# Two attention layers and two Fourier layers on one core: contraction over 192 channels as 128 + 64 rows

## The chip, the cores and the metric

The kernel runs on one core of a Trainium2 chip, in one launch. The metric is the device time of an execution in microseconds (us); of several executions the median is given. A profile is one further execution, taken by the hardware profiler. Engines: PE (TensorE, matmuls; PEld is its weight load), DVE (VectorE), ACT (ScalarE), POOL (GpSimd), SP (SyncE, here only the issuer of copies).

## The reference

An image x of shape (8, 16, 16, 192) goes through four layers. Two attention layers (in the style of a windowed vision transformer), then two layers that mix channels in the Fourier domain. The change touches the attention layers only, one of which is, shortened:

```python
h = layernorm(x) * n1_w + n1_b
win = window_partition(pad(h), 14)                  # 16x16 padded to 28x28: 4 windows of 14x14 = 196 tokens
q, k, v = split(win @ qkv_w + qkv_b)                # 12 heads of 16 channels
attn = (q * 0.25) @ k.T + rel_h[..., None] + rel_w  # relative positions: q @ rel_pos_h, q @ rel_pos_w
out = softmax(attn) @ v
x = x + unpartition(out @ proj_w + proj_b)[:, :16, :16]
mlp = gelu((layernorm(x) * n2_w + n2_b) @ lin1_w + lin1_b) @ lin2_w + lin2_b    # 192 -> 768 -> 192
return x + mlp
```

Padded positions have q, k and v equal to the bias, and as keys they count in the softmax.

## The kernel before, in words

**Jobs and steps.** The eight images are four pairs of 512 tokens. A job is one pair in one attention layer, so there are 8 jobs (layer 0 for jobs 0 to 3, layer 1 for 4 to 7). Within a job the attention runs in 36 steps: 9 units (3 groups of four heads x 3 windows: the two full windows of 196 tokens, and the 120 tokens of the cut windows) of four heads each. The tokens are put in the order of the windows when they are written to SBUF (`pieces`, L135). A step makes scores for one head on PE (`scores`, L911, 8 steps ahead), takes the row maximum on DVE (`row_max`, L516), makes the transposed scores on PE (`scores_T`, L944), exponentials on ACT (`exps`, L707, into PT), and once per unit the values product (`values`, L958), in which four heads use four groups of 32 columns of the array. The maxima of a unit are transposed on PE into bank 5 (`transpose_max`, L934), copied on DVE (`copy_max`, L529) and sent by ACT as one or two small copies into a row of `q_aug` (`send_max`, L744).

**The rest of a job is laid between the steps by hand.** Job m's steps carry the preparation of job m+1 (normalise, transpose, q/k/v projections, relative-position terms) and the end of job m-1 (output projection, second norm, MLP). The step numbers stand in L46 to L57; `build`'s four engine programs (DVE from L590, ACT from L779, PE from L1055, POOL from L421) walk the same step list. All engines are in order, so an instruction that waits holds back everything behind it on its engine. Work between the steps uses two PSUM banks in turn (`free_bank`, L131; `front_free`, L835, waits until a bank's former use is read). Banks 0 and 1 hold scores, 2 and 3 transposed scores, 4 the values product, 5 the transposed maxima and the transposed output.

**Contraction over 192 channels.** Every product over the 192 channels is two matmuls of 96 rows, one of them of 97 where a row of ones adds the bias: `project` (L865; q and k as two tiles of 96 columns each, and in the first job of a layer also the padding keys, `pads_in`, L1038), `values_in` (L900, seven token tiles, the last two or three with padding), `project_out` (L990) and `up` (L1013, six tiles of 128 hidden units). All matmuls with fp32 operands are issued as two instructions, so 8 `project` matmuls stand in the trace as 16 instructions; scores and transposed scores are fp32r and one instruction each.

**Evacuations.** q and k are split into a high and a low part: ACT writes the high part (`q_high`, `k_high`, L656, L664), DVE the difference (`q_low`, `k_low`). POOL adds both again for the relative-position product (`sum_q`, L393; `bias`, L877, 16 matmuls of 32 output rows per axis and group of six heads; `transpose_bias`, L891; `r_high`, `r_low`). ACT writes v (`copy_v`, L698). For the MLP ACT loads the Gelu table, makes two Gelus and loads the Exp table again, three times per job (L796).

**Copies.** SP copies the parts of q, k and of the relative-position terms from their tiles into `q_aug` and `k_aug`, where a head's terms lie on separate partitions, per pair of heads: 4 copies of q, 4 of k, 4 of bias per pair (`send`, L326), 72 per job, and 4 per pair for the padding keys in the first job of a layer. SP first waits until the steps of the former job are done with those heads. The weights for the end of a job are held once for both layers; `load_back(1)` (L274) loads layer 1's after all copies for job 5 and after job 3's last matmuls, and one semaphore counts all seven loads.

**Start and end.** Before job 0's steps the loads, the first norm, the projections and the copies for job 0 run one after another (L342 to L356 on SP); after job 7's steps its own end runs with nothing beside it (L1099). Then the Fourier part (`fourier`, L1116) runs, about 99.5 us; the change doesn't touch it.

Of the kernel before, what the change touches and what calls it, by code (L numbers as in the profile page):

```python
# [6 lines left out]
ALU = mybir.AluOpType  # L7
# [16 lines left out]
G = 2  # L24
HG = NH // G
TILES = TOK // 128
RT = 2 * WS - 1
RK = WS * HG
SUB = HG // 2
# [16 lines left out]
V_AT = (35, 0, 1, 2)  # L46
X_AT = 3
Q_AT, K_AT = (5, 15), (7, 16)
B_AT = ((9, 13), (18, 22))
BT_AT = ((10, 14), (21, 25))  # L50
P_AT = (29, 30)
O_AT = 8
PROJ_AT = (11, 12)
Y_AT = 17
UP_AT = (19, 20, 23, 24, 27, 28)
DOWN_AT = (31, 32, 33, 34)
STATS_AT = (19, 23, 27)  # L57
BIAS_ORDER = ("h a w", "w h a")
V_TILES = [(0, 1), (2, 3), (4, 5), (6,)]
# [17 lines left out]

def first_of_layer(n):
    return n % PAIRS == 0


def free_bank_uses():

    uses = []

    def front(n, wanted):
        uses.extend((n, use) for use in wanted.split())

    pads = lambda n, use: use if first_of_layer(n) else ""
    front(0, "x0 x1 q0 k0 p0 h0 H0 w0 W0 q1 k1 p1 h1 H1 w1 W1 v0")  # L90
    for m in range(JOBS + 1):
        now, more, past = m < JOBS, m + 1 < JOBS, m >= 1
        if now:
            front(m, "v1 v2 v3")
        if more:
            front(m + 1, "x0 x1 q0 k0")
        if past:
            front(m - 1, "t0 t1")
        if more:
            front(m + 1, "h0 H0")  # L100
        if past:
            front(m - 1, "o0 o1")
        if more:
            front(m + 1, "w0 W0 q1 k1")
        if past:
            front(m - 1, "y0 y1")
        if more:
            front(m + 1, "h1")
        if past:
            front(m - 1, "u0 u1")  # L110
        if more:
            front(m + 1, "H1 w1")
        if past:
            front(m - 1, "u2 u3")
        if more:
            front(m + 1, "W1")
        if past:
            front(m - 1, "u4 u5")
        if more:
            front(m + 1, pads(m + 1, "p0 p1"))  # L120
        if past:
            front(m - 1, "d0 d1 d2 d3")
        if more:
            front(m + 1, "v0")
    return uses
# [5 lines left out]
def free_bank(n, use):  # L131
    return 6 + FREE.index((n, use)) % 2
# [34 lines left out]
def attention(nc, d, x_all, bank, consts):  # L167
    with ExitStack() as ctx:
# [3 lines left out]
        def sem(name):  # L172
# [4 lines left out]
        w_qkv = [sb(f"w_qkv{l}", [97, G, 3 * C]) for l in range(2)]  # L177
        w_rel = [sb(f"w_rel{l}", [96, 2 * RT * HG]) for l in range(2)]
        w_proj = sb("w_proj", [97, G, C])
        w_up = sb("w_up", [96, G, MLP])  # L180
# [3 lines left out]
        affine = [sb(f"affine{l}", [96, 4, G]) for l in range(2)]  # L184
# [18 lines left out]
        negT = sb("negT", [8, 4, CUT], F32R)  # L203
# [3 lines left out]
        yT = sb("yT", [97, G, TOK])  # L207
# [6 lines left out]
        names = ("stats1 stats2 aggr1 aggr2 veps1 veps2 rstd1 rstd2 xn1 xn2 xT_mm xT_dve xT_act q_mm q_hi q_lo q_nat "  # L214
                 "k_mm k_hi k_lo p_mm p_hi p_lo r_tok rt_copy r_mm r_hi r_lo v_mm v_copy s_mm max nt_mm negT st_mm exp pv "
                 "o_copy ot_mm inv_sum o_tok oT_mm oT_dve oT_act proj x1 x1b x2_mm x2_dve x2_act up gelu down out").split()
        S = {k: sem(k) for k in names}
        PER = dict(stats1=2, stats2=2, aggr1=1, aggr2=1, veps1=1, veps2=1, rstd1=1, rstd2=1, xn1=1, xn2=1, xT_mm=2,
                   xT_dve=1, xT_act=1, q_mm=2, q_hi=2, q_lo=2, q_nat=2, k_mm=2, k_hi=2, k_lo=2, r_tok=4, rt_copy=4, r_mm=4, r_hi=4, r_lo=4,
                   v_mm=4, v_copy=4, s_mm=STEPS, max=STEPS, nt_mm=UNITS, negT=UNITS, st_mm=STEPS, exp=STEPS,  # L220
                   pv=UNITS, o_copy=UNITS, ot_mm=3, inv_sum=3, o_tok=3, oT_mm=2, oT_dve=1, oT_act=1, proj=2, x1=2, x1b=1,
                   x2_mm=2, x2_dve=1, x2_act=1, up=MC, gelu=MC, down=4, out=4)
        ld_x = [sem(f"ld_x{p}") for p in range(PAIRS)]
        ld_front = [sem(f"ld_front{l}") for l in range(2)]
        ld_static = sem("ld_static")
        ld_back = [sem(f"ld_back{l}") for l in range(2)]
# [4 lines left out]
        q_in = [sem(f"q_in{j}") for j in range(NH // 2)]  # L231
        k_in = [sem(f"k_in{j}") for j in range(NH // 2)]
        r_in = [sem(f"r_in{j}") for j in range(NH // 2)]
        p_in = [sem(f"p_in{j}") for j in range(NH // 2)]
# [3 lines left out]
        PRESETS = 7  # L238
        SENT = 16 * 4
        LD_FRONT, LD_BACK, LD_STATIC = 16 * 4, 16 * 7, 16 * 3  # L240
# [9 lines left out]
        def neg_count(U):  # L250
            return 16 * sum(1 if window(k) == 2 else 2 for k in range(U % 4, U + 1, 4))
# [8 lines left out]
        def _(sp):  # L260
# [6 lines left out]

            def load_front(l):
# [5 lines left out]
            def load_back(l):  # L274
                if l:
                    need(sp, "proj", PAIRS - 1, 2)
# [14 lines left out]
            def rows_of(j, size):  # L291
                return size * (j % SUB), size * (j % SUB) + size
# [1110 lines left out]
```

## Time and profile before

| what | value |
|---|---|
| median of 3 runs | 760.63 us (760.5 to 761.8) |
| the profiled execution's own time | 765.32 us |
| its span, first to last instruction | 763.4 us |
| mean granted TensorE clock | 0.939 of 2.4 GHz |
| PE busy | 650.4 us (85%) |
| DVE, ACT, POOL busy | 351.1, 369.8, 114.9 us |
| bytes moved by copies | 47.4 MB, mean 62 GB/s |

In the profile a row of the timeline gives the start in us from the span's start, the time from the group's first start to its last end, the engine, the line, the operation, the tiles (out<-in), the shape and the count, and in brackets how long the engine had been idle and what released it. PE's matmuls are pipelined: a matmul's own duration is longer than the distance to the next one, so the cost of a stream is read from the length of a group. SPq and ACTq are the issuing of copies by SP and ACT. A row of a stretch gives its window, its length in us, the busy us of each engine (with the instructions it completed where they are given), the granted clock and what the copies moved. The stretches run from the first exponential of one job to that of the next (56.05, 127.77, ..., 412.14, 495.35, 565.60); the last exponential of job 7 ends near 624.

### The profile page before, as it was taken

How to read it: one execution, taken by the hardware profiler on the slowest of the kernel's cores; microseconds unless marked ns; L12 is line 12 of the kernel's file. 1: busy time of each engine (PE TensorE's matmuls, PEld its weight loads, DVE VectorE, ACT ScalarE, POOL GpSimd, SP SyncE). 2: the span in 40 equal slices, each digit the busy share in tenths (PEclk: the TensorE clock that was granted, in tenths of full speed). 3: DMA queues.
4: the chain of work that ended last, by engine and by line, in shares of the span. 5: the costliest groups of instructions: out<-in, count | busy, mean ns of one | idle time of the engine just before them, and what ended most of it. 6: DMA issues, size and time to landing. Idle time of an engine off the chain costs nothing. (4 is left out here: it accounts for less than half of the span.)

```text
span 763.4 us, 15089 instructions
## 1 busy us (share of the span) xinstructions
PE 650.4 (85%) x5592; PEld 486.9 (64%) x5592; DVE 351.1 (46%) x961; ACT 369.8 (48%) x869; POOL 114.9 (15%) x161
## 2 busy tenths in 40 slices
PE   2754598998999999899989598999898877799996
PEld 1333467756875777597659375876597464577774
DVE  3242354654473457335644363356337212156664
ACT  3312254567446555745573336455834741145452
POOL 3120002112020202020220020202001001132231
PEclk9977699999999999999999889999999996989998
DMA  8323233433232135323332522133321000000000
GB/s 207 78 59 91 61 78 81 112 81 70 64 76 66 39 78 133 81 48 76 78 84 48 140 55 60 31 76 79 74 48 40 2 1 0 0 1 22 22 21 21
DMA packets 39342, 47.37 MB, mean 62 GB/s; under 512 B 11852, under 2 KB 20366, under 8 KB 39270
## 3 DMA queue, kind: packets, MB, share of 16 engines
q1 hardware_dynamic: 38310, 46.21, 25.2%
q8 instruction: 46, 0.75, 0.4%
q10 hardware_dynamic: 960, 0.20, 0.1%
q14 instruction: 26, 0.21, 0.1%
HBM read 7.05 MB, written 1.57 MB: 11 GB/s over the span
## 5 line engine op out<-in xcount | busy, mean ns | idle before, releaser
L713 ACT ACTIVATE PT<-bank 98x392 f32<-98x392 f32 (+1 forms) x288 | 136.9, 482 | 179.3 <-PE bank L954 177.8
L525 DVE TENSOR_REDUCE neg_max<-bank 98x2 f32<-98x392 f32 x192 | 105.7, 559 | 70.5 <-PE bank L930 70.0
L954 PE MATMUL bank<-q_aug,k_aug 127*98 127x196 f32 (+1 forms) x672 | 115.2, 265 | 17.9 <-ACT PT L713 16.8
L930 PE MATMUL bank<-k_aug,q_aug 126*98 126x196 f32 x384 | 99.2, 342 | 25.4 <-DMA q_aug<-st_r 15.6
L954 PEld LDWEIGHTS bank<-q_aug,k_aug 127*98 127x98 f32 (+1 forms) x672 | 90.3, 173 | 26.2 <-ACT PT L713 19.7
L1019 PE MATMUL bank<-yT,w_up 96*128 96x512 f32 x192 | 99.7, 649 | 6.6 <-DVE st_r L513 5.6
L930 PEld LDWEIGHTS bank<-k_aug,q_aug 126*98 126x98 f32 x384 | 57.3, 172 | 62.3 <-issue 56.1
L523 DVE TENSOR_REDUCE neg_max<-bank 120x1 f32<-120x318 f32 x96 | 45.7, 484 | 67.1 <-PE bank L926 66.8
L873 PE MATMUL bank<-xT,w_qkv 96*96 96x512 f32 (+3 forms) x144 | 69.5, 611 | 1.9 <-ACT xT L653 1.4
L1028 PE MATMUL bank<-w_down,hidden 128*128 128x192 f32 x384 | 68.9, 331 | 1.0 <-ACT hidden L741 0.9
L391 POOL TENSOR_TENSOR rstd<-veps,half_pow 128x4 f32<-128x4 f32 x16 | 16.4, 1024 | 321.1 <-DVE veps L448 321.1
L1028 PEld LDWEIGHTS bank<-w_down,hidden 128*128 128x128 f32 x384 | 61.7, 190 | 4.2 <-issue 2.2
L968 PE MATMUL bank<-PT,v_aug 98*32 98x196 f32 (+1 forms) x1344 | 63.0, 312 | 0.6 <-ACT PT L713 0.6
L1019 PEld LDWEIGHTS bank<-yT,w_up 96*128 96x128 f32 x192 | 35.7, 204 | 36.3 <-issue 28.5
L513 DVE TENSOR_TENSOR st_r<-bank,st_r 84x392 fp32r<-84x392 f32 (+2 forms) x96 | 26.1, 325 | 67.7 <-ACT st_r L695 67.7
L398 POOL TENSOR_TENSOR q_nat<-st_q 96x392 f32<-96x392 f32 (+2 forms) x48 | 24.9, 545 | 207.5 <-DVE st_q L493 207.5
L759 ACT ACT_TABLE_LOAD x43 | 55.2, 1283 | 0.8
L568 DVE TENSOR_TENSOR x_all<-bank,x_all 128x192 f32<-128x192 f32 x32 | 11.4, 358 | 77.6 <-PE bank L1028 77.6
L926 PE MATMUL bank<-k_aug,q_aug 126*120 126x318 f32 x96 | 46.6, 485 | 0.6 <-DVE neg_max L525 0.4
L907 PE MATMUL bank<-w_qkv,xT 97*98 97x192 f32 (+1 forms) x224 | 44.2, 338 | 0.0
L968 PEld LDWEIGHTS bank<-PT,v_aug 98*32 98x32 f32 (+1 forms) x1344 | 34.3, 110 | 11.2 <-ACT PT L713 1.0
L873 PEld LDWEIGHTS bank<-xT,w_qkv 97*96 97x96 f32 (+1 forms) x144 | 22.8, 176 | 27.7 <-issue 25.5
(87 smaller groups left out, 904.3 us busy)
## 6 DMA issues: line engine op xcount, KB each, us to landing
q_aug<-st_q SPq DMA_DIRECT2D x192, 64.0 KB, 2.0
k_aug<-st_k SPq DMA_DIRECT2D x192, 64.0 KB, 2.0
q_aug<-st_r SPq DMA_DIRECT2D x192, 56.0 KB
x_all<-in_x SPq DMA_DIRECT2D x4, 384.0 KB, 7.2
q_aug<-negT ACTq DMA_DIRECT2D x96, 1.5 KB
out<-y_out SPq DMA_DIRECT2D x4, 384.0 KB, 2.6
k_aug<-st_p SPq DMA_DIRECT2D x48, 24.8 KB, 1.9
w_up<-in_up_w SPq DMA_DIRECT2D x2, 576.0 KB
```

Source lines behind the costliest of these rows:

```text
L523: ins = v.tensor_reduce(neg_max[0:CUT, U % 4, e:e + 1], b[0:CUT, 0:CUT + PADS], AX.X, ALU.max, negate=True)
L525: ins = v.tensor_reduce(neg_max[0:HALF, U % 4, e:e + 5:4], b[0:HALF, 0:2 * WIN] .rearrange("p (r m) -> p r m", r=2), AX.X, ALU.max, negate ...
L713: s.activation(PT[0:rows, s_ % 8, 0:m], bank[2 + s_ % 2][0:rows, 0:m], ACT.Exp).then_inc(S["exp"], 1)
L759: s.activation(spare[:, at:at + 1], spare[:, 0:1], function)
L873: ins = t_.matmul(b[0:96, 0:cols[1] - cols[0]], w_qkv[l][0:rows, part, c0 + 96 * g:c0 + 96 * g + 96], xT[0:rows, part, cols[0]:cols[1]], s ...
L907: last = t_.matmul(b[0:rows, C * k:C * k + C], xT[0:97 - g, g, c0:c0 + rows], w_qkv[l][0:97 - g, g, 2 * C:3 * C], start=(g == 0), stop=(g ...
L926: last = t_.matmul(b[0:CUT, 0:CUT + PADS], q_aug[0:NEG, h, c:c + m], k_aug[0:NEG, h, c:KEYS], start=True, stop=True)
L930: last = t_.matmul(b[0:HALF, WIN * r:WIN * r + WIN], q_aug[0:NEG, h, c + HALF * r:c + HALF * r + HALF], k_aug[0:NEG, h, c:c + WIN], start= ...
L954: last = t_.matmul(b[0:keys, m * k:m * k + m], k_aug[0:NEG + 1, h, c + keys * k:c + keys * k + keys], q_aug[0:NEG + 1, h, c:c + m], start= ...
L968: last = t_.matmul(bank[4][32 * e:32 * e + 32, c:c + m], v_aug[0:rows, t0 + k, head(U, e), :], PT[0:rows, (4 * U + e) % 8, m * k:m * k + m ...
L1019: last = t_.matmul(bank[free_bank(n, f"u{f}")][:, :], w_up[:, g, 128 * f:128 * f + 128], yT[0:96, g, :], start=(g == 0), stop=(g == 1))
L1028: last = t_.matmul(bank[free_bank(n, f"d{t}")][:, 0:C], hidden[:, f, 128 * t:128 * t + 128], w_down[:, f, :], start=(f == 0), stop=(f == M ...
```

## The change

1. **128 + 64 rows.** The 192 channels are held as two tiles of 128 rows that overlap: tile 0 has channels 0 to 127, tile 1 channels 64 to 191. A product is a matmul of 128 rows and a remainder of 64. For even outputs the remainder is rows 64 to 127 of tile 1, for odd outputs rows 0 to 63 of tile 0, and the code issues the two remainders of a pair one behind the other, into different banks. This holds for the projections of q and k, of v, of the output, and for `up`.
2. **q and k in three tiles** of 128 columns (q and k together are 384), in place of four of 96.
3. **Biases in evacuations.** The rows of ones go; ACT and DVE add the bias when they read PSUM (q and k: Identity with a bias; v: a tensor_tensor, moved from ACT to DVE); POOL adds the projection bias to x once per job (`add_proj_bias`, 128x768). Keys and values of the padding are made on DVE from the biases, so their matmuls go. The scale of k is multiplied into the weights on DVE once per layer.
4. **Three free banks** (5, 6, 7). The transposed maxima go into spare columns of the score banks as part of the next unit's first `scores`; the transposed output takes a free bank in turn.
5. **Copies by quads of heads**: 4 + 4 + 4 copies for four heads, 36 per job, each of twice the bytes; the maxima's copy is one per unit for all windows.
6. **Order.** The step numbers move (X from 3 to 2, q and k at 4 and 7, `up` in three steps with its two Gelus in the same step, and so on). The start's loads are reordered: front weights first, the rest of the images and all weights for the end behind the copies of job 0, where `proj_b` is the first of them. `load_back` becomes four loads with semaphores of their own; layer 1's are placed inside job 4.

The core of the diff (semaphore counts, shapes that follow from the above and host-side packing left out):

```diff
+KD = 128
+KR = C - KD
-X_AT = 3
-Q_AT, K_AT = (5, 15), (7, 16)
+X_AT = 2
+AB_AT, C_AT = 4, 7
-UP_AT = (19, 20, 23, 24, 27, 28)
-DOWN_AT = (31, 32, 33, 34)
+UP_AT = (19, 22, 25)
+DOWN_AT = (28, 31, 32, 34)
+def inner(j, part):
+    if j % 2 == 0:
+        return ((0, 0, KD), (1, KR, KD))[part]
+    return ((1, 0, KD), (0, 0, KR))[part]
...
-    return 6 + FREE.index((n, use)) % 2
+    return 5 + FREE.index((n, use)) % 3
...
 def send_queries(n, j):
+    tile, row = divmod(64 * j, 128)
     for z in range(2):
         for r in (2 * z, 2 * z + 1):
-            load(q_aug[r:BIAS:4, 2 * j:2 * j + 2, :].bitcast(F32), st_q[a:b, g, z, :].bitcast(F32), q_in[j])
+            load(q_aug[r:BIAS:4, 4 * j:4 * j + 4, :].bitcast(F32), st[row:row + 64, tile, z, :].bitcast(F32), q_in[j])
...
 load_x(0)
 load(ident[:, :], d["ident"], ld_static)
+load_front(0)
+load_rel(0)
 load(cls[:, :], d["q_class"], ld_static)
 load(k_static[64:128, :], d["k_static"], ld_static)
-load_front(0)
 load_x(1)
-load_back(0)
-for p in (2, 3):
-    load_x(p)
 sp.wait_ge(cls_done, 1)
 load(q_aug[CLASS:CLASS + 6, :, :].bitcast(F32), cls_r[:, :].bitcast(F32).unsqueeze(1).to_broadcast([6, NH, TOK]), cls_in)
-send(0, (0, 1, 2), 0)
...
+for j in range(QUADS):
+    send(0, j)
+for p in (2, 3):
+    load_x(p)
+load_proj_bias(0)
+load_proj(0)
+load_up(0)
+load_down(0)
 for m in range(JOBS):
     if m + 1 < JOBS:
-        send(m + 1, (0, 1), 12)
-        send(m + 1, (2, 3), 24)
-        send(m + 1, (4, 5), STEPS)
+        send(m + 1, 0)
+        if m == PAIRS:
+            load_proj(1)
+        send(m + 1, 1)
+        if m == PAIRS:
+            load_up(1)
+            load_down(1)
+        send(m + 1, 2)
...
+def add_proj_bias(n):
+    need(pool, "xn1", n, 1)
+    pool.wait_ge(ld_bias[layer(n)], 16)
+    g_.tensor_tensor(x(n), x(n), b_proj[:, :].unsqueeze(1).to_broadcast([128, TILES, C]), ALU.add)\
+        .then_inc(S["xb"], 1)
 rsqrt(1, 1)
 normalise(1)
+add_proj_bias(0)
+add_proj_bias(1)
 for m in range(JOBS + 1):
     more, past = m + 1 < JOBS, m >= 1
     if more:
         sum_q(m + 1, 0)
+        sum_q(m + 1, 1)
...
+def project(n, tiles):
+    l = layer(n)
+    for part in range(2):
+        for j in tiles:
+            if part == 0:
+                front_free(n, f"a{j}")
+                need(pe, ("xT_dve", "xT_act")[j % 2], n, 1)
+            elif j == 2:
+                need(pe, "xT_act", n, 1)
+            tile, r0, r1 = inner(j, part)
+            last = t_.matmul(bank[free_bank(n, f"a{j}")][:, :], w_qkv[l][r0:r1, tile, 128 * j:128 * j + 128],
+                             xT[r0:r1, tile, 0:TOK], start=(part == 0), stop=(part == 1))
+    last.then_inc(S["a_mm"], 1)
...
 def scores(s):
...
     need_all(pe, "max", s - 1)
+    if e == 2:
+        need_all(pe, "negT", U)
...
+    if e == 0 and U >= 1:
+        last = transpose_max(U - 1)
     last.then_inc(S["s_mm"], 1)
...
-def up(n, f):
-    for g in range(G):
-        last = t_.matmul(bank[free_bank(n, f"u{f}")][:, :], w_up[:, g, 128 * f:128 * f + 128], yT[0:96, g, :],
-                         start=(g == 0), stop=(g == 1))
+def up(n, k):
+    tiles = (2 * k, 2 * k + 1)
+    for part in range(2):
+        for f in tiles:
+            if part == 0:
+                front_free(n, f"u{f}")
...
+            tile, r0, r1 = inner(f, part)
+            last = t_.matmul(bank[free_bank(n, f"u{f}")][:, :], w_up[r0:r1, tile, 128 * f:128 * f + 128], yT[r0:r1, tile, :],
+                             start=(part == 0), stop=(part == 1))
     last.then_inc(S["up"], 1)
```

`values_in` and `project_out` issue their matmuls in the same way: for each part, for each token tile of a bank, for both banks. The v projection is done in two steps (35 for four tiles, 1 for two) in place of four.

## Rows read from the trace of the kernel before

**Rows 1.** stretches of jobs 0, 1, 5, 6, 7: length, busy us, clock.

```profile
56.05:127.77 71.72, 49.42 (x503) 37.65 (x503) 28.54 (x76) 27.68 (x73) 8.11 (x11) 0.81 0.33 77
127.77:198.00 70.23, 66.29 (x635) 50.41 (x634) 35.77 (x101) 40.45 (x97) 10.94 (x13) 1.00 0.33 79
...
412.14:495.35 83.21, 71.12 (x635) 54.26 (x634) 35.95 (x101) 40.29 (x97) 10.93 (x13) 0.90 0.31 73
495.35:565.60 70.25, 66.26 (x635) 50.41 (x634) 34.35 (x92) 40.46 (x96) 5.93 (x8) 1.00 0.28 66
565.60:624.47 58.87, 52.09 (x436) 39.82 (x434) 23.69 (x63) 32.59 (x72) 2.84 (x2) 0.97 0.11 26
```

**Rows 2.** PE's waits over the whole span; us in total, times, longest.

```profile
PE bank L954 <- ACT PT L713: 16.8, 14, 1.6
PE bank L930 <- DMA q_aug<-st_r: 15.6, 1, 15.6
...
PE bank L1000 <- DMA w_down<-in_down_w: 8.4, 1, 8.4
```

**Rows 3.** timeline of PE in job 6, steps 18 and 19.

```profile
526.65 0.60 PE L978 MATMUL bank<-ident,o_nat 128*128 128x128 f32 x4
527.18 0.79 PE L887 MATMUL bank<-w_rel,q_nat 96*32 96x84 f32 x32
527.90 0.42 PE L930 MATMUL bank<-k_aug,q_aug 126*98 126x196 f32 x2
528.16 0.35 PE L954 MATMUL bank<-q_aug,k_aug 127*98 127x196 f32 x2
528.35 1.90 PE L1019 MATMUL bank<-yT,w_up 96*128 96x512 f32 x4
```

**Rows 4.** timeline of PE: a v projection and a values product.

```profile
200.28 1.55 PE L907 MATMUL bank<-w_qkv,xT 97*106 97x192 f32 x8
...
549.54 0.87 PE L968 MATMUL bank<-PT,v_aug 98*32 98x196 f32 x16
```

**Rows 5.** timeline of job 6 behind its second pair of Gelus.

```profile
542.87 1.28 ACT L759 ACT_TABLE_LOAD   x1
...
544.27 0.47 ACT L713 ACTIVATE PT<-bank 98x392 f32<-98x392 f32 x1
...
544.79 0.43 PE L954 MATMUL bank<-q_aug,k_aug 127*98 127x196 f32 x2 [1.25 <-ACT PT L713]
```

**Rows 6.** timeline of SP's issues at the start.

```profile
9.95 2.47 SPq L262 DMA_DIRECT2D q_aug<-rt  x1
23.32 7.62 SPq L262 DMA_DIRECT2D q_aug<-st_q  x12
30.98 8.37 SPq L262 DMA_DIRECT2D k_aug<-st_k  x12
39.39 10.13 SPq L262 DMA_DIRECT2D q_aug<-st_r  x12
49.56 8.15 SPq L262 DMA_DIRECT2D k_aug<-st_p  x12
```

**Rows 7.** timeline of DVE at the start: the first low part of q.

```profile
22.60 0.69 DVE L493 TENSOR_TENSOR st_q<-bank,st_q 96x512 fp32r<-96x512 f32 x1 [4.68 <-ACT st_q L662]
```

**Rows 8.** copies: KB each, median us from issue to landing.

```profile
q_aug<-st_q SPq DMA_DIRECT2D x192, 64.0 KB, 2.0
...
x_all<-in_x SPq DMA_DIRECT2D x4, 384.0 KB, 7.2
...
k_aug<-st_p SPq DMA_DIRECT2D x48, 24.8 KB, 1.9
```

**Rows 9.** groups of POOL and DVE by form; busy us, mean ns.

```profile
L404 POOL TENSOR_TENSOR x_all<-x_all,b_down 128x768 f32<-128x768 f32 x8 | 14.6, 1823 | 20.7 <-DVE xn L478 20.7
...
L554 DVE TENSOR_TENSOR x_all<-bank,x_all 128x384 f32<-128x384 f32 x16 | 8.9, 553 | 18.4 <-PE bank L1000 18.3
```

More of the change, by code:

```diff
@@ L84, in free_bank_uses, with add @@
     uses = []
[L86 to L90, printed above, removed]
+    def add(n, wanted):
+        if 0 <= n < JOBS:
+            uses.extend((n, use) for use in wanted.split())
+    add(0, "x0 x1 a0 a1 a2 h0 H0 w0 W0 h1 H1 w1 W1 v0 v1")
     for m in range(JOBS + 1):
[L92 to L124, printed above, removed]
+        if m < JOBS:
+            add(m, "v2 v3")
+        add(m + 1, "x0 x1 a0 a1")
+        add(m - 1, "z2")
+        add(m + 1, "a2")
+        add(m - 1, "t0 t1")
+        add(m + 1, "h0 H0")
+        add(m - 1, "o0 o1")
+        add(m + 1, "w0 W0 h1 H1 w1")
+        add(m - 1, "y0 y1")
+        add(m, "z0")
+        add(m - 1, "u0 u1")
+        add(m + 1, "W1")
+        add(m - 1, "u2 u3 u4 u5 d0")
+        add(m, "z1")
+        add(m - 1, "d1 d2 d3")
+        add(m + 1, "v0 v1")
     return uses
@@ L250, in neg_count, with max_bank @@
         def neg_count(U):
-            return 16 * sum(1 if window(k) == 2 else 2 for k in range(U % 4, U + 1, 4))
+            return 16 * (U // 4 + 1)
+        def max_bank(U):
+            return (4 * U + 4) % 2
         def columns(U):
@@ L427, in _ @@
                     add_down_bias(m - 1)
-                if more:
-                    sum_q(m + 1, 1)
                 if m + 2 < JOBS:
@@ L633, in _ @@
             copy_oT(last)
-            add_proj(last, 0)
-            second_stats(last, 0)
-            add_proj(last, 1)
-            second_stats(last, 1)
+            for j in range(2):
+                add_proj(last, j)
+            for j in range(2):
+                second_stats(last, j)
             normalise(last)
@@ L853, in front_free, with transpose_rows @@
                 else:
-                    need(pe, {"v": "v_copy", "o": "x1", "u": "gelu", "d": "out"}[kind], m, j + 1)
+                    need(pe, {"a": "a_lo", "v": "v_copy", "o": "x1", "u": "gelu", "d": "out", "z": "o_tok"}[kind], m, j + 1)
+            def transpose_rows(n, uses, rows, done):
+                for g, use in enumerate(uses):
+                    front_free(n, use)
+                    b = bank[free_bank(n, use)]
+                    for t in range(TILES):
+                        last = t_.transpose(b[:, 128 * t:128 * t + 128], rows(t)[:, KR * g:KR * g + KD], ident[:, :])
+                    last.then_inc(S[done], 1)
@@ L856, in transpose_x @@
             def transpose_x(n):
                 need(pe, "xn1", n, 1)
-                for g in range(G):
-                    front_free(n, f"x{g}")
-                    b = bank[free_bank(n, f"x{g}")]
-                    for t in range(TILES):
-                        last = t_.transpose(b[0:96, 128 * t:128 * t + 128], xn[:, 0, t, 96 * g:96 * g + 96], ident[:, :])
-                    last.then_inc(S["xT_mm"], 1)
-            def project(n, use, cols, c0, done):
-                l, g = layer(n), int(use[1])
-                front_free(n, use)
-                need(pe, "xT_dve", n, 1)
-                need(pe, "xT_act", n, 1)
-                b = bank[free_bank(n, use)]
-                for part in range(2):
-                    rows = 97 - part
-                    ins = t_.matmul(b[0:96, 0:cols[1] - cols[0]], w_qkv[l][0:rows, part, c0 + 96 * g:c0 + 96 * g + 96],
-                                    xT[0:rows, part, cols[0]:cols[1]], start=(part == 0), stop=(part == 1))
-                ins.then_inc(S[done], 1)
+                transpose_rows(n, ("x0", "x1"), lambda t: xn[:, 0, t, :], "xT_mm")
```

633 lines of the change are left out of this document (317 added, 316 removed).

## The prediction

> **What bounds the kernel now.** I read the windows from one job's first exponential to the next's, then PE's waits, then timelines inside a job. In a steady job (1 or 6) PE is busy 66.3 of 70.2 us at full clock, while DVE has 36, ACT 40 and POOL at most 11 [rows 1]: PE sets the time there, and about 4 us per job are its idle time. Job 0 and job 5 are the exceptions. Job 0 has 49.4 us of work for PE in 71.7; one wait of 15.6 us for copies of bias terms lies in it. Job 5 has the work of its neighbours and is 13 us longer; one wait of 8.4 us for `w_down` is in it, and the clock there is 0.90 [rows 1, 2].
>
> What a matmul costs is the length of its group. Four fp32 instructions of 512 columns last 1.90 us, and a group outlasts the distance to its successor by about 0.17 (528.35 begins 0.19 after a pair that is given 0.35), so an instruction is (1.90 - 0.17)/4 = 0.43 and a matmul, two of them, 0.86 [rows 3]. For 192 columns the same gives (1.55 - 0.17)/8 = 0.17 and 0.33 to 0.35 a matmul [rows 4].
>
> The profiled execution took 765.3 us (span 763.4), 4.7 above the median of the runs; the sum is made against 765.3 and 4.7 is taken off at the end. A measurement can tell about 0.2%, 1.5 us.
>
> **The change, part by part.**
>
> *Remainders.* Counted in slots of one matmul, if two remainders on different halves of the rows run side by side: q and k go from 8 to 5 (three full, one pair, one single), `up` from 12 to 9, both at 0.86; the output projection from 8 to 6, v from 14 (seven tiles) to 9 (six full, three pairs), at 0.33. That is 2.58 + 2.58 + 0.66 + 1.65 = 7.5 us less PE time per job. That they run side by side no row shows for rows. For columns one does: in the values product 16 instructions of 196 columns take 0.87 us, (0.87 - 0.17)/16 = 0.044 each, against 0.17 alone, so four column groups do run together although the two instructions of each matmul stand next to each other [rows 4]. Bounds: the 7.5, or, if nothing overlaps, 7.5 less six pairs (3 + 1 at 0.86, 5 at 0.33: 5.1) = 2.4. I take 7.5, as the nearest row is about the same array split the other way.
>
> The Trainium skill ("TensorE: Matmul & The Clock Gate", section "Part 3: Packing small matmuls — row/col tiling") says that matmuls keep program order in start and in end. Taken strictly, a pair issued as high, low, high, low would need three instruction slots and not two; the values row above speaks against it.
>
> *Switching the array.* Work in small tiles amid work of the whole array has a price. Four transposes last 0.60, so 0.43 by the correction of 0.17, but 0.53 pass until the 32-row bias block behind them begins; that block lasts 0.79, so 0.62, but 0.72 pass until the next scores [rows 3]. Each border costs 0.10, an excursion 0.20, and I round that up to 0.25. The new pairs make some 8 excursions per job (two in q/k, three in `up`, two in v, one in the projection): +2.0. Bounds 0 and twice that.
>
> *Gelus.* Two `up` tiles now land in one step with both Gelus and two table loads (1.28 us for one, [rows 5]) as before, but there is less other PE work laid between a block of Gelus and the next scores that need an exponential. Now such a block leaves PE idle for 1.25 us [rows 5], 1.2 us on average over 14 waits [rows 2]. I add 0.6 us for each of three blocks, +1.9; bounds 0 (PE's pieces still cover it) and +3.
>
> So a steady job changes by -7.5 + 2.0 + 1.9 = -3.5, and six of them (1 to 6) by **-21**, bounds -36 and -6. Covered by other engines: DVE takes v with its bias from ACT, four instructions of about 0.55 by a like one [rows 9], under 3 us on an engine with 34 idle; POOL adds the projection bias, 1.82 by the same operation for another bias [rows 9], on an engine with 59 idle; ACT only loses work. These cost nothing while PE bounds; if PE fell under 45 they would show. SP issues 36 instead of 72 copies per job; 72 at 0.71 are 51 of its 70 us.
>
> *The start.* 48 copies are issued between 23.3 and 57.7, 0.71 each [rows 6], after the first low part of q [rows 7], and 48 more behind them. After the change 48 are all. What one of twice the bytes costs no row shows: below, as now 0.63 (q, 64 KB, [rows 6, 8]); above, 2.47 for `q_aug<-rt` [rows 6]. The copies of the padding keys have under half the bytes of q's and cost 0.68, no less [rows 6, 8], so I take an unchanged price. Quad 0's twelve are then issued by 23 + 8.6 = 32. Now the fourth bias copy is issued by 43 and the first exponential comes 13 later, at 56; so it would come near 45. The wait of 15.6 [rows 2] goes, since the other quads follow 12 us apart from 32 on, ahead of PE. What is late next is `b_proj`: POOL's two `add_proj_bias` for pairs 0 and 1 wait for it, and `sum_q` for job 1 is queued behind them, on which PE's `bias` at step 9 depends. It is loaded behind 48 copies (done at 23 + 34 = 57) and two of x; x takes 7.2 to land [rows 8], so it is there at about 66, then 2 x 1.82 and one sum of the same size [rows 9]: 71. PE reaches step 9 at 45 + 9 x 1.56 = 59 (job 0 without its wait: 56.1 over 36 steps). It stalls some 12 us, and the 27 steps left, at 1.56 less the thinner work of the front, take 40: job 1 begins near 111 in place of 127.8. **-16**, bounds -27 (bias lands before PE needs it) and -10 (each copy 0.13 dearer).
>
> *The layer change.* Layer 1's four loads are issued inside job 4, each with its own semaphore. Both waits of job 5 go, and job 5 is like job 6: 83.2 - 70.25 = **-13**, bounds -13 and -8.
>
> *The rest.* Padding keys' matmuls for two layers, four of about 0.34: **-1**. Job 7 has the projection, v and `up` but no front, half of the gain less the switching: **-2**. Its end runs alone: six slots of `up` become fewer by three (2.6) and the projection by two (0.7): **-3**. `k`'s scaling on DVE, the padding's keys and values made there, once per layer: beside other work, nothing.
>
> Sum: -21 - 16 - 13 - 1 - 2 - 3 = -56; 765.3 - 56 = 709.3, less 4.7: **705**. With bounds that aren't all met at once, 690 to 720.
>
> **Rivals.**
> *Remainders in strict order* (three instruction slots): a pair of 512 columns costs 0.43 more, one of 192 columns 0.17; four and five of these per job are 2.6 us, over seven jobs 18: 723. The values row [rows 4] speaks against it. Chance 0.08.
> *Remainders one after another* (the change doesn't do what it says): 5.1 per job, over seven jobs and a bit 37: 742. No row-split product is in the trace to exclude it. 0.10.
> *Copies by bytes*: a copy of twice the size costs twice the issue, 1.43. The start is then as long as now (48 x 1.43 = 69, +34): 739. Later jobs have 36 x 1.43 = 51 of 67, as now. Speaks against it: the padding copies [rows 6]. 0.08. The Trainium skill ("Perfetto Trace Analysis", section "What "DMA-bound" means") takes the issuing engine's busy window as descriptor generation, which would scale with what a copy is cut into; by that rule this rival's price holds, but the padding copies disagree.
> *SP becomes the bound* (the slower side): each quad copy costs what `q_aug<-rt` does, 2.47 [rows 6], whose destination spans all heads. Then 36 x 2.47 = 89 us per job against 67 of PE, and the start is 84 longer: 705 + 84 + 6 x 22 = 920. It decides from 1.9 us per copy: 36 x 1.9 is a job, and 48 x 1.2 = 57 in the start eats the whole gain. For it: the only copy across many heads is the dearest. Against: that one is a broadcast of six rows, and q's price is the same for three pairs on different rows. 0.07.
>
> **How the numbers follow.** Forecast 0.67, the rivals 0.08, 0.10, 0.08, 0.07. The time is the forecast's, 705. The range runs from 690 to 745: it takes in the three rivals on the faster side and leaves out the slow one and the outer tails. All but the last are faster by over 0.2%: 0.91, with 0.02 for a mishap that ends at no change; slower 0.07.
>
> **What would show it.** Right: groups of `up` for two tiles of about 2.8 us (eight instructions: 4 full at 0.43, then four in the time of two), against 3.6 if nothing overlaps and 3.2 in strict order; job periods near 67; the first exponential near 45; one wait of PE in job 0 near 59 to 71 for relative-position work behind POOL; none for `w_down`; copies of q of 128 KB issued at 0.6 to 0.8. Wrong: copies above 1 us each; waits for exponentials behind Gelus of over 2 us in each block; a clock below full in a steady job, which now is 1.00 [rows 1]; PE waiting for a bank of the three in turn, which a slow evacuation on DVE would cause.

## The result and the profile after

The changed kernel takes 727.5 us (four runs, 726.9 to 728.2) against 761.2: a ratio of 0.956, 95% interval 0.954 to 0.957, 34 us less. Forecast were 56 us less (705, range 690 to 745). The profiled execution took 727.2, its span is 725.3, so the two traces differ by 38.1 us in span; 4 of that is the long execution of before, which took 765.3 where the median is 761.2.

The same windows as in [rows 1] for the changed kernel: jobs 0, 1, 2, 5, 6 and 7 (length, busy us of PE, PEld, DVE, ACT and POOL, granted clock, copies).

```profile
48.61:104.57 55.96, 43.51 (x493) 31.99 (x492) 30.55 (x86) 25.82 (x68) 13.44 (x14) 0.91 0.43 141
104.57:177.51 72.94, 65.90 (x625) 47.85 (x625) 38.57 (x110) 39.39 (x91) 12.75 (x14) 0.95 0.23 73
177.51:247.27 69.76, 62.69 (x625) 45.45 (x625) 40.28 (x117) 39.39 (x91) 10.91 (x13) 1.00 0.20 67
...
390.28:461.83 71.55, 64.48 (x625) 46.05 (x625) 38.49 (x110) 39.40 (x90) 12.75 (x14) 0.98 0.22 69
461.83:533.62 71.79, 64.55 (x625) 46.07 (x625) 37.11 (x101) 39.38 (x91) 5.92 (x8) 0.98 0.19 65
533.62:591.20 57.58, 49.19 (x424) 35.98 (x424) 26.08 (x71) 31.99 (x68) 2.82 (x2) 0.97 0.07 22
```

| stretch | before | after | measured | forecast |
|---|---|---|---|---|
| start to the first exponential, and job 0 | 127.8 | 104.6 | -23.2 | -16 |
| jobs 1 to 4 and 6 | 354.6 | 357.5 | +2.9 | -17.5 |
| job 5 | 83.2 | 71.6 | -11.7 | -13 - 3.5 |
| job 7 to its last exponential, its end and the Fourier part | 197.8 | 191.7 | -6.1 | -6 |

The start gave more than forecast and the end what was forecast. The steady jobs, from which 21 us were to come, gave nothing: job 6 had 66.3 us of PE work in 70.25 and now has 64.6 in 71.8, at a clock of 0.98 in place of 1.00. Not every job of before was at 1.00, though. Job 2 of before (and job 3 likewise) was not:

```profile
198.00:269.77 71.77, 67.96 (x635) 51.20 (x634) 35.77 (x101) 40.46 (x97) 10.93 (x13) 0.98 0.28 65
```

PE's waits over the whole span; beside them stand [rows 2].

```profile
PE bank L1004 <- ACT PT L755: 26.4, 20, 1.8
...
PE bank L888 <- DVE xn L505: 10.2, 7, 5.2
PE bank L988 <- DVE neg_max L570: 8.3, 9, 1.8
PE bank L925 <- issue: 7.1, 1, 7.1
```

The waits for bias copies and for `w_down` are gone. The wait of transposed scores (L1004, before L954) for exponentials has grown from 16.8 to 26.4, and three that were not there or small have come: for the second norm's rows (L888; 5.2 of its 10.2 lie in the end of job 7, where 4.3 were waited before, and 0.9 in each of jobs 1 to 6), for the last maximum of a unit, whose transposes now stand in the next unit's first `scores` (L988), and the forecast one of job 0 for POOL (L925).

**The matmuls.** PE and its weight loads in job 6: the third q/k tile, the output projection, two tiles of `up`, its remainders alone, and v.

```profile
474.08 2.10 PE L906 MATMUL bank<-xT,w_qkv 128*128 128x512 f32 x4
...
476.11 0.42 PE L978 MATMUL bank<-k_aug,q_aug 126*98 126x196 f32 x2
476.37 0.25 PE L988 MATMUL bank<-ident,neg_max 98*66 98x98 f32 x1
...
481.42 2.37 PE L1049 MATMUL bank<-w_proj,yT 128*128 128x192 f32 x16
...
495.10 2.96 PE L1069 MATMUL bank<-yT,w_up 128*128 128x512 f32 x8
...
495.98 0.19 PEld L1069 LDWEIGHTS bank<-yT,w_up 128*128 128x128 f32 x1 [0.24 <-issue]
496.93 0.30 PEld L1069 LDWEIGHTS bank<-yT,w_up 64*128 64x128 f32 x4 [0.76 <-issue]
...
496.93 1.13 PE L1069 MATMUL bank<-yT,w_up 64*128 64x512 f32 x4
...
530.65 2.32 PE L952 MATMUL bank<-w_qkv,xT 128*98 128x192 f32 x16
```

Four instructions of two remainders last 1.13 us. One after another they would need 4 x 0.43 + 0.17 = 1.89, in strict order 1.46; two lengths are 1.03. So they run side by side, with a loss of 0.1. Another 0.1 is lost at the entry, and that one has its sign in the weight loads: a 128-row matmul's weights are loaded ahead of it (495.98 for the matmul that starts at 496.40), those of the first two remainder instructions start with them at 496.93, PEld having stood idle for 0.76 us. (The second two are loaded at 497.03 and start at 497.46, so a late load is not what the 0.1 between the halves comes from; its cause is not shown.) A remainder without a partner costs as much: from 474.08 to the next scores 2.03 us pass for four instructions of 0.43, which is 0.31 too much.

### The profile page after: what moved, and what is told of

Read it like the earlier page. It is cut to its first block and busy times, and to the rows that moved or that the text cites. A ratio compares the mean times of both kernels' runs of the same rounds, so it can differ in the third digit from the quotient of the medians.

```text
span 725.3 us, 14493 instructions
## 1 busy us (share of the span) xinstructions
PE 616.3 (85%) x5512; PEld 442.5 (61%) x5512; DVE 373.2 (51%) x1043; ACT 358.9 (49%) x825; POOL 131.7 (18%) x169
## 5 line engine op out<-in xcount | busy, mean ns | idle before, releaser
L1004 PE MATMUL bank<-q_aug,k_aug 127*98 127x196 f32 (+1 forms) x672 | 112.7, 261 | 26.4 <-ACT PT L755 26.4
L1004 PEld LDWEIGHTS bank<-q_aug,k_aug 127*98 127x98 f32 (+1 forms) x672 | 88.7, 170 | 31.1 <-ACT PT L755 19.1
L978 PE MATMUL bank<-k_aug,q_aug 126*98 126x196 f32 x384 | 82.5, 298 | 7.2 <-DVE neg_max L572 4.7
L978 PEld LDWEIGHTS bank<-k_aug,q_aug 126*98 126x98 f32 x384 | 52.0, 168 | 44.8 <-issue 27.7
L1069 PE MATMUL bank<-yT,w_up 128*128 128x512 f32 (+1 forms) x192 | 79.0, 664 | 0.1
L419 POOL TENSOR_TENSOR q_nat<-st 128x392 f32<-128x392 f32 (+5 forms) x48 | 26.7, 589 | 141.4 <-DVE st L539 141.4
L1069 PEld LDWEIGHTS bank<-yT,w_up 128*128 128x128 f32 (+1 forms) x192 | 26.1, 203 | 38.3 <-issue 37.2
L783 ACT ACTIVATE hidden<-bank,b_up 128x512 f32<-128x512 f32 x48 | 30.4, 683 | 35.0 <-PE bank L1069 35.0
L562 DVE TENSOR_TENSOR st_r<-bank,st_r 112x392 fp32r<-112x392 f32 (+5 forms) x96 | 26.1, 324 | 39.3 <-ACT st_r L746 38.7
L906 PE MATMUL bank<-xT,w_qkv 128*128 128x512 f32 (+1 forms) x96 | 43.7, 665 | 0.7 <-DVE xT L515 0.5
L974 PE MATMUL bank<-k_aug,q_aug 126*120 126x318 f32 x96 | 37.1, 387 | 2.5 <-DVE neg_max L570 1.5
L888 PE MATMUL bank<-ident,xn 128*128 128x128 f32 x128 | 19.6, 301 | 22.0 <-POOL xn L432 11.8
```

The lines of the kernel that those rows point to most:

```text
L783: s.activation(hidden[:, f, :], bank[free_bank(n, f"u{f}")][:, :], ACT.Gelu, bias=b_up[:, f:f + 1])\
L906: last = t_.matmul(bank[free_bank(n, f"a{j}")][:, :], w_qkv[l][r0:r1, tile, 128 * j:128 * j + 128], xT[r0:r1, tile, 0:TOK], start=(part == ...
L974: last = t_.matmul(b[0:CUT, 0:CUT + PADS], q_aug[0:NEG, h, c:c + m], k_aug[0:NEG, h, c:KEYS], start=True, stop=True)
L978: last = t_.matmul(b[0:HALF, WIN * r:WIN * r + WIN], q_aug[0:NEG, h, c + HALF * r:c + HALF * r + HALF], k_aug[0:NEG, h, c:c + WIN], start= ...
L1004: last = t_.matmul(b[0:keys, m * k:m * k + m], k_aug[0:NEG + 1, h, c + keys * k:c + keys * k + keys], q_aug[0:NEG + 1, h, c:c + m], start= ...
L1069: last = t_.matmul(bank[free_bank(n, f"u{f}")][:, :], w_up[r0:r1, tile, 128 * f:128 * f + 128], yT[r0:r1, tile, :], start=(part == 0), sto ...
```

## The experiments

**Remainders that do not stand next to each other.**

```diff
-for part in range(2):
-    for f in tiles:
+for f in tiles:
+    for part in range(2):
```

(the same in `project`, `values_in` and `project_out`)

> The changed kernel with every remainder issued right behind its own 128-row matmul, so that no two remainders stand next to each other. Theory (two remainders on different halves of the rows run side by side; a change between the whole array and a part of it costs about 0.3 us in the changed kernel's groups): 5.1 us more per job for the pairs and up to 9 borders more, 2.7 us; over seven jobs and the end 37 to 58 us more than 727.5, so 765 to 785. The group of `up` for two tiles goes from 2.9 us to 3.4 or more. Rival (the pairs bring nothing, the gain came from the start and the layer change alone): 727, within 3 us.

Measured: 841.3, ratio to the kernel before 1.106 (1.102 to 1.111). Its job 6 and one `up` of two tiles:

```profile
526.84:612.27 85.43, 78.97 (x625) 50.82 (x625) 37.23 (x101) 39.39 (x90) 5.93 (x8) 0.90 0.17 55
...
563.85 4.20 PE L1066 MATMUL bank<-yT,w_up 128*128 128x512 f32 x8
```

The pairs do bring their gain; the rival is out. The miss upward (841 where 765 to 785 were expected) is in job 6 the clock: 0.10 of 85.4 us is 8.5 us, against 1.7 in the changed kernel's job 6 (worked out below), and without both the jobs differ by 76.9 - 70.1 = 6.8 us, where 5.1 to 7.8 were expected. So half of what this job lost is the clock. `up` takes 4.2 in place of 2.96, more than the 0.86 of the lost overlap: one more way into a remainder and out of it stands in it, which leaves 0.38 for that.

**The single remainder on all rows.** Half of its weights are zero.

```diff
+v.memset(w_qkv[l][0:64, 1, 256:384], 0.0).then_inc(S["scaled"], 1)
...
+if j == 2:
+    r0, r1 = 0, KD
```

> The changed kernel with the single remainder of the third q/k tile as a matmul of all 128 rows, half of its weights set to zero once per layer. Theory (a remainder costs its slot and about 0.3 us for the change of the array's shape): its group goes from 2.03 to about 1.72 us, 0.3 us less per job, 2 us in all: 725. Rival (the 0.3 us is in the group for another reason): the group stays at 2.0 and the time within 1 us of 727.5.

Measured: 724.5 (0.954; 0.950 to 0.957), so by the times alone it can't be told from the changed kernel (0.956; 0.954 to 0.957). Its trace does tell:

```profile
470.87 1.90 PE L910 MATMUL bank<-xT,w_qkv 128*128 128x512 f32 x4
...
472.79 0.25 PE L992 MATMUL bank<-ident,neg_max 98*66 98x98 f32 x1
...
458.97:530.08 71.11, 64.07 (x625) 46.24 (x625) 37.15 (x101) 39.33 (x90) 5.93 (x8) 0.98 0.20 66
```

The group takes 1.90, as four 512-column instructions did before [rows 3]. Behind whole-row matmuls the next scores show an early start (472.21, where the group lasts to 472.77), so I count to what stands behind both scores, the transpose of the maxima: 470.87 to 472.79 is 1.92, and 2.29 in the changed kernel (474.08 to 476.37). Job 6 is 0.7 us shorter, jobs 2 to 4 are so by 0.2 to 0.4, where 0.3 was expected. A lone remainder thus costs its slot and 0.3 to 0.4 us for the change of shape. (Jobs 1 and 5 are 1.8 and 1.9 us shorter, with one fall of the clock less each, and job 0 is 2.0 longer; of job 0 more below.)

**`b_proj` first.** Its load stands ahead of job 0's copies. In the changed kernel SP, POOL and PE show there:

```profile
22.09 2.56 SPq L267 DMA_DIRECT2D q_aug<-st  x4
25.28 2.45 SPq L267 DMA_DIRECT2D k_aug<-st  x4
30.47 5.12 SPq L267 DMA_DIRECT2D q_aug<-st_r  x4
...
37.13 4.22 PE L952 MATMUL bank<-w_qkv,xT 128*98 128x192 f32 x16
...
62.53 0.50 SPq L267 DMA_DIRECT2D b_proj<-in_proj_b  x1
...
66.71 3.56 POOL L439 TENSOR_TENSOR x_all<-x_all,b_proj 128x768 f32<-128x768 f32 x2 [20.94 <-DMA b_proj<-in_proj_b]
...
71.88 1.72 PE L925 MATMUL bank<-w_rel,q_nat 128*32 128x112 f32 x32 [7.07 <-issue]
```

> The changed kernel with `b_proj` of layer 0 loaded ahead of job 0's copies. Theory: PE's wait of 7.1 us in job 0 is POOL's wait for `b_proj`, and nothing else is late there: 6 to 7 us less, 721. Rival: another thing is late in the same place (SP's copies for job 1, the low part of q) and the wait only changes its name: less than 2 us gained.

Measured: 722.9 (0.950; 0.947 to 0.954). Job 0 goes from 56.0 to 52.7 and the first exponential from 48.6 to 47.5: 4.4 of the 7.1. The wait is gone, as the theory has it. The rest goes to the same 493 matmuls, 46.4 us busy for 43.5, at a granted clock of 0.89 in place of 0.91. That leaves the result between theory and rival, and the size of the gain uncertain: in the traces of four runs below and above whose edits leave job 0 as it is, or nearly so, job 0 takes 56.1, 58.0, 58.9 and 59.7 us at clocks of 0.92, 0.89, 0.86 and 0.84, so a single trace of job 0 tells no more than some 4 us.

**All six Gelus in one step.**

```diff
-UP_AT = (19, 22, 25)
+UP_AT = 19
...
-    f = 2 * UP_AT.index(k)
-    gelu(m - 1, f)
-    gelu(m - 1, f + 1)
+    for f in range(MC):
+        gelu(m - 1, f)
```

What it is against stands in job 6 of the changed kernel, ACT and PE around the second and third pair of Gelus:

```profile
504.78 1.26 ACT L783 ACTIVATE hidden<-bank,b_up 128x512 f32<-128x512 f32 x2 [0.48 <-PE bank L1069]
506.06 1.28 ACT L795 ACT_TABLE_LOAD   x1
507.35 0.20 ACT L795 ACTIVATE spare<-spare 1x1 f32<-1x1 f32 x1
...
507.96 0.43 PE L1004 MATMUL bank<-q_aug,k_aug 127*98 127x196 f32 x2 [1.61 <-ACT PT L755]
508.31 1.04 PE L1018 MATMUL bank<-PT,v_aug 106*32 106x120 f32 x24
509.29 4.47 PE L1069 MATMUL bank<-yT,w_up 128*128 128x512 f32 x8
...
517.16 0.40 PE L1004 MATMUL bank<-q_aug,k_aug 127*98 127x196 f32 x2 [1.80 <-ACT PT L755]
```

Two Gelus, a table load and its first use take 2.8 us behind each `up`; PE has a few scores to do and then waits 1.6 and 1.8. Behind the first gap the clock falls, and the next `up` takes 4.47 where 495.10 shows 2.96. The windows of PE there (length, busy, granted clock):

```profile
506.00:507.00 1.00, 0.34 (x3) 1.00 0.31 107
507.00:508.00 1.00, 0.04 (x1) 1.00 0.53 191
508.00:509.00 1.00, 1.00 (x26) 0.89 0.62 211
509.00:512.50 3.50, 3.50 (x12) 0.54 0.53 181
```

That is 0.11 + 3.5 x 0.46 = 1.7 us lost at 1.2 GHz, in jobs 3 to 6 once and in job 1 twice; job 2, where the clock is 1.00, is 1.7 us shorter than job 3 with the same work. Not every such gap is followed by a fall: job 2 has one of 1.6 us (223.25) and one of 1.8 (230.62) at 1.00 throughout, and behind the gap of 1.80 in job 6 the clock stays at 1.00 too.

> The changed kernel with the three `up` steps and all six Gelus in step 19, with two table loads per job in place of six. Theory (a job loses 4.0 us behind Gelus and then 1.5 us to the half clock that follows): one stall of about 2 us remains, the clock stays at 1.00, 3 us less per job over six jobs: 709, between 704 and 718. Rival 1 (the period is set by DVE and ACT, which starve during 8.7 us of `up`): the steps behind it wait for them, no gain or up to 2 us more per job: 727 to 740. Rival 2 (the half clock has nothing to do with these waits): granted clock still 0.98 in the jobs, and about 12 us gained.

Measured: 718.8 (0.944; 0.941 to 0.947), 9 us less, half of what was expected. Its waits and DVE's line behind the Gelus:

```profile
PE bank L977 <- DVE neg_max L572: 13.1, 16, 1.4
...
502.97 0.81 DVE L562 TENSOR_TENSOR st_r<-bank,st_r 56x392 fp32r<-56x392 f32 x3 [2.32 <-ACT st_r L746]
...
456.95:526.15 69.20, 64.22 (x625) 46.61 (x625) 37.24 (x101) 33.86 (x82) 5.92 (x8) 0.98 0.20 67
```

The waits for exponentials have left the list's head. In their place DVE, in order, waits for the high part of a bias term that ACT has queued behind six Gelus, and the row maxima behind it are late. The clock still falls. So rival 1 is right about a new wait, not about its size.

**The same with the last bias block moved behind `up`.**

```diff
-B_AT = ((9, 12), (14, 16))
-BT_AT = ((10, 13), (15, 20))
+B_AT = ((9, 12), (14, 20))
+BT_AT = ((10, 13), (15, 23))
```

> As the run with all `up` in step 19, and the second relative-position block of the third quad moved behind it: its product from step 16 to 20, its transposes from 20 to 23. Theory (what was left of the stall there, 0.5 us for an exponential and 1.4 us for a maximum, comes from DVE's low part at step 20, which waits for ACT's high part queued behind the six Gelus, and the half clock of 1.7 to 5 us per job follows those gaps): both gaps go, the clock stays near 1.00, 66 to 67.5 us per job, 704, between 698 and 709. Rival (8.9 us without scores starve DVE and ACT whatever stands behind): jobs stay at 69.3 us, 717 to 720.

Measured: 710.0 (0.932; 0.929 to 0.935). Jobs 1 and 6:

```profile
107.26:174.92 67.66, 62.62 (x625) 45.48 (x625) 38.63 (x110) 33.50 (x82) 12.76 (x14) 1.00 0.24 79
...
450.99:519.14 68.15, 62.87 (x625) 45.47 (x625) 37.29 (x101) 33.49 (x82) 5.92 (x8) 1.00 0.21 68
```

Both gaps are gone and the clock is 1.00 in four of six jobs. The theory holds in those four; in jobs 2 and 3 the clock is 0.98 still. The six jobs take 68.6 us on average where 66 to 67.5 were expected: the normalised rows for `up` are now waited for 1.7 us per job, 0.8 more than in the changed kernel. Job 0, which the edit leaves alone, is 3.0 us longer in this trace, and job 7 is 4.1 shorter.

**Filling the gaps.** The one run that leaves Gelus, tables and order alone.

```diff
+if past and k in (25, 28):
+    filler(STEPS * m + k, m - 1, "u4" if k == 25 else "d0")
 scores_T(STEPS * m + k)
```

> The changed kernel with twelve matmuls of 120 columns, whose output nobody reads, ahead of the transposed scores of steps 25 and 28 of each job from the second, where PE now waits 1.6 and 1.8 us for an exponential behind Gelus. The Gelus, their table loads and the order are as they were. Theory (the half clock of 1.7 us per job, three quarters of the jobs, follows from these gaps and costs by itself): the gaps are filled, the clock stays at 1.00, 1.7 us less in jobs 1 (twice) and 3 to 6: 9 to 10 us, 718. Rival 1 (the half clock comes from something else, the narrow matmuls for one): granted clock still 0.98, 727 to 729. Rival 2 (the filler itself outlasts the gap): slower by up to 1 us per job.

Measured: 721.9 (0.943; 0.938 to 0.948). Jobs 1 and 5:

```profile
107.97:177.79 69.82, 64.81 (x649) 47.72 (x649) 38.51 (x110) 39.44 (x91) 12.75 (x14) 1.00 0.24 77
...
389.94:459.75 69.81, 64.76 (x649) 47.68 (x649) 38.52 (x110) 39.45 (x90) 12.73 (x14) 1.00 0.23 71
```

Job 5 goes from 71.55 to 69.81 and job 1 from 72.94 to 69.82 by 24 matmuls whose output nobody reads. Jobs 1 and 3 to 6 are all at 1.00 and together 9.8 us shorter, as the theory has it: in these jobs the half clock goes with the gaps, and it has a price of its own, 1.7 us a time. Job 2 went the other way (72.4 at 0.98). Another gap is left there, 1.8 us for a row maximum (230.96) that stands behind the scaling of layer 1's weights on DVE (228.52); the clock falls behind it here and did not in the changed kernel. Why one gap is followed by a fall and another is not stays open. The whole gained 5.6 us where 9 to 10 were expected. In the trace 3.9 are left of the 9.8, since job 2 takes back 2.7 and the start with job 0, which holds no filler, 3.4. (Beside this run the kernel before took 765.3, and 761.2 beside the changed kernel, so by the ratios, 0.943 and 0.956, the gain is 9 us.)

**Twice as many copies of half the size.**

```diff
-load(q_aug[r:BIAS:4, 4 * j:4 * j + 4, :].bitcast(F32), st[row:row + 64, tile, z, :].bitcast(F32), q_in[j])
+for i in range(2):
+    load(q_aug[r + 32 * i:32 * i + 32:4, 4 * j:4 * j + 4, :].bitcast(F32),
+         st[row + 32 * i:row + 32 * i + 32, tile, z, :].bitcast(F32), q_in[j])
...
```

> The changed kernel with each copy of q, k, bias and padding keys cut in two by partitions: as many copies as before the change, 96 in the start and 72 per job. Theory (a copy's issue costs 0.64 to 0.85 us whatever it holds): the copies in the start take 33 us more to issue, the first exponential comes 8 us later, `b_proj` 33 us later, and PE's wait for POOL in job 0 takes up the rest: 760, between 752 and 765; later jobs are as long as now. Rival (the price goes with the bytes): at most 8 us more, 728 to 736.

Measured: 778.2, slower than the kernel before (1.023; 1.018 to 1.028). SP's first copies and its `b_proj`, and jobs 0 and 3:

```profile
22.01 5.76 SPq L267 DMA_DIRECT2D q_aug<-st  x8
...
33.52 6.55 SPq L267 DMA_DIRECT2D q_aug<-st_r  x8
...
94.76 0.50 SPq L267 DMA_DIRECT2D b_proj<-in_proj_b  x1
...
48.97:139.24 90.27, 52.01 (x493) 37.17 (x492) 30.65 (x86) 26.10 (x68) 13.45 (x14) 0.70 0.27 93
...
284.52:366.30 81.78, 66.53 (x625) 47.81 (x625) 38.52 (x110) 39.50 (x90) 14.48 (x15) 0.92 0.24 82
```

A copy is issued in 0.72 us with half the bytes, 0.64 with all of them (22.09 above). `b_proj` comes 32 us later and job 0 is 34 us longer, with two waits of PE in it: 16.6 us for POOL behind `b_proj`, where the changed kernel has 7.1, and 12.0 for the bias copies of the next quad, like the 15.6 of before [rows 2]. One part of the expectation failed: the first exponential comes 0.4 us later and not 8, although quad 0's last bias copy is issued at 40.1 and not at 35.6. So those copies do not set it in the changed kernel: after 35.6 PE is at the v projection until 41.3, at a low clock (37.13 takes 4.22 us where 530.65 shows 2.32), and goes on to the first scores without a wait. The expectation for the later jobs holds for 4 to 6 (71.5 to 71.8). Beyond the expectation job 3 is 10 us longer. The mechanism is that of job 0: layer 1's `b_proj` is queued on SP behind 72 copies, is issued 17 us into the job (301.86), and PE waits 8.3 us for POOL's sums.

**Layer 1's loads late**, behind all copies for job 5; then the same with half copies.

```diff
 send(m + 1, 0)
-if m == PAIRS:
-    load_proj(1)
 send(m + 1, 1)
-if m == PAIRS:
-    load_up(1)
-    load_down(1)
 send(m + 1, 2)
+if m == PAIRS:
+    load_proj(1)
+    load_up(1)
+    load_down(1)
```

> The changed kernel with layer 1's loads for the end of a job placed behind all copies for job 5, as before the change; each still has its own semaphore. Theory (the place of the loads made the waits of job 5): the waits for `w_proj` and `w_down` come back, 8 to 13 us more, 736 to 740. Rival (one semaphore for seven loads made them, and with one each they land in time): within 3 us of 727.5.

> Both earlier edits at once: twice as many copies of half the size, and layer 1's loads behind all copies for job 5. Theory (neither the place of the loads nor their semaphores made the wait of job 5, but how long SP still issues copies when job 5 begins: 24 copies then, 12 now): the loads are issued some 16 us into job 5, PE waits 5 to 9 us for weights in it, and job 5 takes 77 to 82 us, against 71.5 with either edit alone. Rival (semaphores of their own are what removed the wait): job 5 stays at 71.5. The whole is then 778 to 790 or 778.

Measured: 732.9 (0.961; 0.955 to 0.966, which overlaps the changed kernel's) and 776.5 (1.016; 1.008 to 1.024). Of the second, SP's first load for the projection, and job 5:

```profile
454.15 0.91 SPq L267 DMA_DIRECT2D w_proj<-in_proj_w  x2
...
438.95:510.62 71.67, 64.60 (x625) 46.10 (x625) 38.52 (x110) 39.46 (x91) 12.74 (x14) 0.98 0.25 88
```

In the first, job 5 takes 71.46 us and PE waits for no weights; its trace is of the fastest of four executions (725.6 to 735.9), and what made the others longer is not shown. In the second the loads go out 15.2 us into job 5, and still PE waits for none: `w_proj` lands at 456.7, 1.6 us before the projection begins (458.34), and `w_down` at 462.5, 4 us behind that. My theory of both runs is out and the rival's mechanism right (its time, within 3 us of 727.5, was missed by 2): a wait for `w_proj` alone, in place of one for all seven loads, is enough to remove the wait for `w_down`. That the place in job 4 brings anything, these runs don't show.

**All that helped, together**: `b_proj` first, the single remainder on all rows, `up` in one step with the block behind it, and

```diff
-if k == Y_AT - 1:
+if k == Y_AT - 2:
     normalise(m - 1)
```

> Four edits together: `b_proj` ahead of job 0's copies, the third tile's remainder on all rows, `up` in one step with the third quad's second block behind it, and DVE's second normalisation in step 15 in place of 16. Theory: -4.6 (measured alone), -2 to -3 (measured alone), -20 to -26 (as expected of the first run of this call) and 0.85 us per job for the wait for the normalised rows, -6: 692, between 685 and 700. Rival (the gaps only move to the next late thing, as for the first edit where 7.1 us of wait gave 4.6): 705 to 715.

Measured: 689.75, 0.906 of the kernel before (0.903 to 0.909), 38 us below the changed kernel. Jobs 0, 1 and 6:

```profile
48.16:98.15 49.99, 42.94 (x493) 32.04 (x492) 30.74 (x86) 25.52 (x68) 10.82 (x13) 0.94 0.55 155
98.15:163.85 65.70, 62.31 (x625) 45.66 (x625) 38.37 (x110) 33.39 (x83) 12.77 (x14) 1.00 0.25 81
...
431.64:498.97 67.33, 64.06 (x625) 47.35 (x625) 37.02 (x101) 33.45 (x82) 5.92 (x8) 0.97 0.21 69
```

The expectation holds in its time (685 to 700). Job 1 is a little below what the prediction had for a steady job of the changed kernel (66.7); jobs 4 and 6 are at 67.3 and job 2 at 69.1, where the clock is 0.97 to 0.98.

## Why the prediction was right, and where it was wrong

The direction and the range held; the time was 22 us too low. That the range held is in part luck: the sum's own bounds were 690 to 720, and only the three rivals on the faster side, none of which came, had stretched the range to 745. The 22 us are 25 that the steady jobs did not give, less 7 that the start gave beyond its term, and 4 to 5 because I took off the 4.7 of the long execution of before at the end: the changed kernel's profiled execution was not a long one (727.2, median 727.5).

*Steady jobs, -3.5 each: failed.* They changed by +0.7 each: 2.9 over five, and 71.55 in job 5 against the 70.25 that I had set for it without its waits, 4.2 in all, outside the bounds of -36 and -6. (Those bounds were also narrower than those of the parts, which reach from -7.5 to +4.6 per job.) By the busy and idle times of the stretches, of the 25 us about 10 are PE's work, 8 its idle time and 7 the clock. By the step's own parts:
- Slots, -7.5: right in count (the nine pairs that the prediction adds up are called six there); side by side, as the values row [rows 4] said. Strict order and no overlap are both excluded by the row of 1.13 us; a run without overlap took 114 us more, in its job 6 half of it by the clock. The Trainium skill ("TensorE: Matmul & The Clock Gate", section "Part 3: Packing small matmuls — row/col tiling") has matmuls in program order; four instructions in 1.13 us don't agree with the strict reading that I gave it.
- Switching, +2.0 for 8 excursions: too small. The single remainder costs 2.03 - 4 x 0.43 = 0.31 to the next scores and 0.37 against the same group on all rows; eight of 0.31 to 0.37 are 2.5 to 3.0. Work at full clock fell from 66.3 to 62.7 (job 2), by 3.6 and not by 5.5; of the 1.9 between, 0.5 to 1.0 are thus the excursions. The rest I have not separated.
- Gelus, +1.9: the wait grew by 1.7 (2.3 to 4.0 in job 6). But all idle time grew from 4.0 to 7.2: the maxima's transposes in the score banks and the second norm's rows bring about 0.9 each, and neither was in the sum.
- The clock: not in the sum at all. It stood only among what would prove me wrong. 1.7 us in four of six jobs and 3.4 in one, 10 in all, less some 3 that jobs 2 and 3 of before had too. The claim that the clock of a steady job was 1.00 before came from jobs 1 and 6 alone. Its price stood in [rows 1]: of the 13 us of job 5, 8.4 are the one wait and 4.9 the same work at a lower clock (71.12 us busy for 66.26).

*The start, -16: -23, in its upper part of the range.* The first exponential came at 48.6 and not 45. Quad 0's bias copies were done issuing at 35.6 and not 32, since they wait for DVE's low parts (30.47; a copy itself takes 0.8 to 0.9), but the run with half copies shows that they do not set the first exponential: PE's v projection at the low clock stands before the first scores. So the path that I had for it, copies and 13 us more, was not the one that held. The wait for `b_proj` came where it was forecast, 64.8 to 71.9, and was 7.1 and not 12. The 27 steps behind it took 33 us where I had 40. Copies cost 0.61 to 0.85 as before: the terms' price was right, and the run with half copies shows that in the new order of loads the gain hangs on their number: without it job 0 ends 11 us later than before the change.

*The layer change, -13: right, half the reason.* Job 5 is as long as job 6 (71.55 and 71.79), where it was 13.0 longer; its -11.7 in the table has the +1.3 of a steady job in it. (The prediction speaks of both waits of job 5; the rows show one.) The semaphores did it; the loads' place in job 4, which the prediction named beside them, was not needed.

*The rest, -6: -6.1.* Of the rivals, copies by bytes, strict order and no overlap are out by rows; SP as the bound did not come: a quad copy costs 0.61 to 0.85 and not 1.9, and the copy from whose 2.47 that rival's price came is issued in 0.93 in the changed kernel (10.20). The run with 72 copies per job shows where SP would tell first, at the small loads that are queued behind them. No run takes back the third bank or the biases in the evacuations by themselves, so what these are worth is not shown.

## What to carry to other kernels

Where PE is 94% busy, time saved in it goes first to what was hidden behind it: work out what gaps each removed piece leaves, and for each gap two prices, the wait and the half clock that may follow it. Before splitting a contraction into tiles of part of the array, count the changes of shape as well as the slots; a lone remainder may be cheaper on all rows with zero weights. And when the number of copies falls, expect the gain at the start, where their issuing is the path, not in the steady part.

## What the runs showed of the hardware that was not expected

Weights of a 64-row matmul behind a 128-row one were loaded with it, not ahead of it (496.93 both), and 0.1 us was lost there; 0.3 to 0.4 us was lost over a whole remainder or pair. The granted clock fell after gaps of 0.2 and 1.6 us and cost 1.7 us each time; after like gaps in job 2, and after one of 1.80 in job 6, it did not fall. With unpaired remainders it stayed at 1.2 GHz for longer, 8.5 us lost in a job, behind gaps like the changed kernel's (23.9 us for exponentials against 26.4): why it stayed low there was not tried.
